# Rows ordered by expert, early lower gathers, and late tiles' results added onto base rows already stored in the output

## What is computed

```python
h = layernorm(x) * (1 + ca) + sa                      # sa .. gb: silu(c) @ wmod, six rows per batch
x = x + ga * rwkv_block(h)                            # time mix (K, V, R, O) and channel mix (key, silu, value)
h = layernorm(x) * (1 + cb) + sb
xt = h.reshape(2048, 512)
shared = sum_e gelu(xt @ Wsh_up[e]) @ Wsh_down[e]     # 2 shared experts, 512 -> 256 -> 512
probs = softmax(xt @ W_router)                        # 16 experts
top_v, top_i = top_k(probs, 2)
routed = sum_e gate[:, e] * (gelu(xt @ Wrt_up[e]) @ Wrt_down[e])
x = x + gb * (shared + routed)
```

## Time and profile before

| | us |
|---|---|
| median of 3 runs | 951.47 |
| the three runs | 957.27, 951.47, 950.63 |
| the profiled execution | 955.24 |
| its span, first to last instruction | 953.5 |
| granted TensorE clock, mean | 0.977 of 2.4 GHz |

### The profile page before, as it was taken

One profiled execution on the slowest core, in us unless ns is written; L12 is line 12 of the kernel. 1 busy time (PEld: TensorE's weight loads), 2 busy tenths in 40 slices (PEclk: granted clock), 3 DMA queues, 4 the chain that ended last, 5 costly groups with the idle time before them and its releaser, 6 DMA issues.

```text
span 953.5 us, 13516 instructions
## 1 busy us (share of the span) xinstructions
PE 894.7 (94%) x4264; PEld 720.3 (76%) x4265; DVE 531.9 (56%) x985; ACT 383.8 (40%) x632; POOL 382.5 (40%) x280
## 2 busy tenths in 40 slices
PE   7899779999998999998999999999999999999993
PEld 2457658788776888887888788878887888888772
DVE  5897897987657111356136513551684444444478
ACT  2566555573745542321222113225452333333441
POOL 2332200100022547227102610369527599897373
PEclk9899979999998999999999999999999999999997
DMA  9548578466056336153114411465435788776576
GB/s 357 188 132 263 193 221 262 156 202 195 1 189 213 109 109 205 40 166 131 55 34 152 135 67 34 162 229 177 161 126 180 249 262 271 237 275 235 163 256 203
DMA packets 105632, 166.69 MB, mean 175 GB/s; under 512 B 8152, under 2 KB 53208, under 8 KB 102512
## 3 DMA queue, kind: packets, MB, share of 16 engines
q1 hardware_dynamic: 59472, 112.59, 34.7%
q0 software_dynamic: 8960, 34.61, 11.4%
q10 hardware_dynamic: 37152, 18.88, 6.7%
HBM read 98.63 MB, written 67.42 MB: 174 GB/s over the span
## 4 chain that ended last, share of the span: by engine, by line
PE 70%; DVE 13%; DMA 6%; issue 4%; ACT 3%; POOL 2%; SPq 1%; another core or an unknown queue 1%; DVEq 0%; ACTq 0%
PE kk_ps L422 6%; PE kv_ps L422 6%; PE kk_ps L424 6%; PE kk_ps L423 6%; PE kv_ps L424 6%; PE kv_ps L423 6%; PE mm_ps L422 4%; PE mm_ps L423 4%; PE mm_ps L424 4%; PE up_ps L422 3%; DMA xsb<-xs_s 3%; PE dn_ps L422 2%; PE dn_ps L424 2%; PE dn_ps L423 2%; PE up_ps L423 2%
## 5 line engine op out<-in xcount | busy, mean ns | idle before, releaser
L1555 DVE TENSOR_TENSOR silu<-kk_ps,silu 128x512 fp32r<-128x512 f32 x64 | 44.2, 691 | 207.6 <-ACT silu L2162 193.2
L2158 ACT ACTIVATE kk_ps<-kk_ps 128x512 f32<-128x512 f32 x64 | 37.2, 582 | 214.9 <-PE kk_ps L424 199.9
L422 PE MATMUL kk_ps<-xk,cm_w 128*128 128x512 f32 x256 | 101.4, 396 | 0.0
L422 PE MATMUL kv_ps<-cm_w,silu 128*128 128x512 f32 x256 | 100.6, 393 | 0.0
L424 PE MATMUL kk_ps<-xk,cm_w 128*128 128x512 f32 x256 | 100.2, 391 | 0.0
L423 PE MATMUL kk_ps<-xk,cm_w 128*128 128x512 f32 x256 | 100.1, 391 | 0.0
L424 PE MATMUL kv_ps<-cm_w,silu 128*128 128x512 f32 x256 | 99.7, 390 | 0.0
L423 PE MATMUL kv_ps<-cm_w,silu 128*128 128x512 f32 x256 | 99.6, 389 | 0.0
L2325 POOL TENSOR_TENSOR cm_w<-stage,cm_w 128x1024 fp32r<-128x1024 f32 x16 | 38.7, 2424 | 90.4 <-ACT cm_w L1946 71.6
L2332 POOL TENSOR_TENSOR rs<-mv,neghalf 128x4 f32<-128x4 f32 (+2 forms) x13 | 13.5, 1038 | 145.3 <-DVE mv L1266 145.2
L2381 POOL TENSOR_TENSOR rs<-mv,neghalf 128x1 f32<-128x1 f32 x16 | 16.1, 1009 | 138.5 <-DVE mv L1580 138.5
(11 more groups left out here) (277 smaller groups left out, 2345.9 us busy)
## 6 DMA issues: line engine op xcount, KB each, us to landing
xs_s<-zero ACTq DMA_DIRECT2D x13, 1024.0 KB, 6.2
xsb<-xs_s SPq DMA_DIRECT2D x44, 256.0 KB, 4.0
ys_s<-ysb SPq DMA_DIRECT2D x41, 256.0 KB, 3.4
ex_raw<-in_wex POOLq DMA_DIRECT2D x9, 1024.0 KB
stage<-in_wcm SPq DMA_DIRECT2D x16, 512.0 KB, 3.9
wmod<-in_wmod SPq DMA_DIRECT2D x6, 1024.0 KB, 9.7
ex_raw<-in_wex SPq DMA_DIRECT2D x6, 1024.0 KB, 5.8
stage<-in_wtm SPq DMA_DIRECT2D x10, 512.0 KB, 6.3
```

The source lines that it names most:

```text
L422: pe.matmul(out, lhs[0], rhs[0], start=first, stop=False)
L1555: dve.tensor_tensor(silu[:, g % NSILU, 1, :], kk_ps[g % 2][:, :], silu[:, g % NSILU, 0, :].bitcast(F32), ALU.subtract).then_inc(s_silo, 1)
L2158: act.activation(kk_ps[g % 2][:, :], kk_ps[g % 2][:, :], ACT.Silu).then_inc(s_silu, 1)
```

## The change

1. The two rows of a token are ordered by expert instead of by rank: VectorE computes `spos` and reorders the gates (`by_expert`), from the kept first choices `top1`.
2. `last_tiles` writes how many increments the two store semaphores have when all tiles of experts 0 to 14 are stored. GpSimd waits for those and gathers the lower expert's rows of tiles 0 to 7 before `s_end`; after `s_end` the upper rows of tiles 0 to 7, then the lower rows of 8 to 15, then (after the first `up` block of batch 3) the upper rows of 8 to 15. ScalarE's `scaled` waits for a whole group of eight lower gathers (`gathered_lower`), VectorE for the tile's upper one.
3. `x4` of tiles 8 to 15 is stored in the output itself; the loads into `bsb` and VectorE's addition of it go, and each of these tiles leaves by an adding transfer from GpSimd. SyncE stores tiles 0 to 7 and at the end waits for those transfers.
4. All of `ys_s` is cleared: eight more clears of 1 MB, one in each of the steps g = 12 to 19 of the channel mix; the waits of SyncE and GpSimd on them count all 26.
5. The orders on ScalarE and VectorE in the tail are new.

The diff, without the buffers' declarations:

```diff
@@ -463,7 +460,10 @@
...
             before = 32 * NB if i < TT else 0 if i < TT + 2 else 16 * (NE - PRE) // 2
-            return before + 32 * (t // NG + 1)
+            return before + 16 * (t // NG + 1)
+
+        def gathered_lower(t):
+            return (s_base, 16 * (SB * TT + NG)) if t < NG else (s_bsl, 16 * (NB + NG))
...
@@ -728,7 +728,8 @@
...
                 sp.wait_ge(s_x4, t + 1)
-                sp.dma_start(x4_s[t], x4b[:, t % TT]).then_inc(s_x4st[t % TT], 16)
+                rows = x4_s[t] if t < SB * TT else out_d[t]
+                sp.dma_start(rows, x4b[:, t % TT]).then_inc(s_x4st[t % TT], 16)
...
@@ -802,7 +803,7 @@
...
             scatters_landed(NB - 1)
-            sp.wait_ge(s_zero, 16 * (2 * NSX - FULL) // 4)
+            sp.wait_ge(s_zero, 16 * 2 * NSX // 4)
             sp.wait_ge(s_tab, 1)
...
@@ -842,10 +843,11 @@
...
             sp.sem_inc(s_end, 1)
-            for t in range(NT):
+            for t in range(SB * TT):
                 sp.wait_ge(s_o4, t + 1)
                 sp.dma_start(out_d[t], g1b[:, t]).then_inc(s_out, 16)
-            sp.wait_ge(s_out, 16 * (NB + NT))
+            sp.wait_ge(s_out, 16 * (NB + SB * TT))
+            sp.wait_ge(s_bsl, 16 * (NB + NG + NT - SB * TT))
...
@@ -1618,8 +1620,9 @@
...
                 done(dve.tensor_tensor(lg[:, 1], lg[:, 1], per_expert(rev[:, :], TT), ALU.mult))
-                done(dve.tensor_reduce(top1[:, :], lg[:, 1], AX.X, ALU.max))
-                done(dve.tensor_tensor(oh[:, c], per_expert(rev[:, :], TT), per_token(top1[:, :], TT), ALU.is_equal))
+                first = top1[:, c, b * TT:(b + 1) * TT]
+                done(dve.tensor_reduce(first, lg[:, 1], AX.X, ALU.max))
+                done(dve.tensor_tensor(oh[:, c], per_expert(rev[:, :], TT), per_token(first, TT), ALU.is_equal))
...
@@ -1750,8 +1753,42 @@
...
                 done(dve.reciprocal(gates[:, 0], tops[:, :]))
-                dve.tensor_tensor(gates[:, 1].rearrange("p (t a) -> p t a", a=1), pr[:, :, NE:NE + 1],
-                                  gates[:, 0].rearrange("p (t a) -> p t a", a=1), ALU.mult).then_inc(s_gates, 1)
+                done(dve.tensor_tensor(gates[:, 1].rearrange("p (t a) -> p t a", a=1), pr[:, :, NE:NE + 1],
+                                       gates[:, 0].rearrange("p (t a) -> p t a", a=1), ALU.mult))
+
+            def by_expert():
+
+                w = pr[:, :, :].rearrange("p t e -> p (t e)")
+                lower, upper_ = w[:, 0:NT], w[:, NT:2 * NT]
+                at, p, q, o = (w[:, (2 + 2 * i) * NT:(4 + 2 * i) * NT].rearrange("p (c t) -> p c t", c=2)
+                               for i in range(4))
+
+                def both(v):
+                    return v.rearrange("p (a t) -> p a t", a=1).to_broadcast([P, 2, NT])
+
+                def ordered(v, out):
+                    own.up(dve.tensor_tensor(p, v, both(lower), ALU.mult))
+                    done(dve.tensor_tensor(q, v, both(upper_), ALU.mult))
+                    own.up(dve.tensor_tensor(out[:, 0], p[:, 0], q[:, 1], ALU.add))
+                    done(dve.tensor_tensor(out[:, 1], q[:, 0], p[:, 1], ALU.add))
+
+                dve.wait_ge(s_pos, NB)
+                own.up(dve.tensor_copy(at, pos[:, :, :]))
+                done(dve.tensor_tensor(lower, top1[:, 0], top1[:, 1], ALU.is_gt))
+                done(dve.tensor_scalar(upper_, lower, -1.0, 1.0, ALU.mult, ALU.add))
+                ordered(at, o)
+                own.up(dve.tensor_copy(spos[:, :, :], o))
+                ordered(gates[:, :, :], gates[:, :, :])
+
+            def last_tiles():
+
+                x = tends[0:1, NE - 2:NE - 1]
+                done(dve.tensor_scalar(total[:, :], x, 0.5, -0.25, ALU.mult, ALU.add))
+                done(dve.tensor_scalar(total[:, :], total[:, :], 8388608.0, None, ALU.add))
+                done(dve.tensor_scalar(total[:, :], total[:, :], -8388608.0, None, ALU.add))
+                done(dve.tensor_tensor(ecol[0:1, 0:1], x, total[:, :], ALU.subtract))
+                own.up(dve.tensor_scalar(tend[:, NE + 1:NE + 2], ecol[0:1, 0:1], 16.0, 16.0, ALU.mult, ALU.add))
+                dve.tensor_scalar(tend[:, NE + 2:NE + 3], total[:, :], 16.0, 16.0, ALU.mult, ALU.add)                    .then_inc(s_gates, 1)
...
@@ -1835,6 +1872,8 @@
...
             gates_b()
+            by_expert()
+            last_tiles()
             gb_shared(TT)
...
@@ -1882,6 +1921,7 @@
...
                 dve.wait_ge(s_o1, t + 1)
+                dve.wait_ge(s_gat[t % NG], gathered(t))
                 if t == 0:
...
@@ -1895,12 +1935,14 @@
...
                     dve.wait_ge(s_gsh, t + 1)
-                dve.wait_ge(s_bsl, 16 * (NT - SB * TT + NB))
+                dve.wait_ge(s_bsl, 16 * NB)
                 if t == 0:
                     dve.wait_ge(s_base, 16 * SB * TT)
-                base = base8[:, t] if t < SB * TT else bsb[:, t - SB * TT]
+                if t >= SB * TT:
+                    dve.tensor_tensor(g1b[:, t], g1b[:, t], gb2[:, b], ALU.mult).then_inc(s_o4, 1)
+                    return
                 done(dve.tensor_tensor(g1b[:, t], g1b[:, t], gb2[:, b], ALU.mult))
-                dve.tensor_tensor(g1b[:, t], g1b[:, t], base, ALU.add).then_inc(s_o4, 1)
+                dve.tensor_tensor(g1b[:, t], g1b[:, t], base8[:, t], ALU.add).then_inc(s_o4, 1)
...
@@ -1910,19 +1952,19 @@
...
             ht_lo(3, [0, 1])
+            combine([0])
             mid_lo(10)
             ht_lo(3, [2, 3])
-            combine([0])
+            combine([1])
             mid_lo(11)
-            combine([1, 2, 3, 4])
+            combine([2, 3, 4, 5, 6, 7])
             mid_lo(12)
-            combine([5])
             mid_lo(13)
-            combine([6])
+            combine([8])
             mid_lo(14)
-            combine([7])
+            combine([9])
             mid_lo(15)
-            combine(range(8, NT))
+            combine(range(10, NT))
...
@@ -2025,7 +2067,7 @@
...
-            groups = [(xs_s, q) for q in range(0, NSX, 4)] + [(ys_s, q) for q in range(FULL, NSX, 4)]
+            groups = [(xs_s, q) for q in range(0, NSX, 4)] + [(ys_s, q) for q in range(NSX - 4, -1, -4)]
...
@@ -2188,6 +2230,8 @@
...
                     weight_hi(14 + g)
+                elif 18 + g - 12 < len(groups):
+                    clear_slots(18 + g - 12)
                 if b and m in (4, 5):
...
@@ -2266,24 +2310,25 @@
...
                 for t in tiles:
-                    act.wait_ge(s_gat[t % NG], gathered(t))
+                    act.wait_ge(*gathered_lower(t))
                     act.activation(g1b[:, t], g1b[:, t], ACT.Copy, scale=gates[:, 0, t:t + 1]).then_inc(s_o1, 1)
-            gelu(2, [0, 1])
+            gelu(2, [0])
+            scaled([0, 1])
+            gelu(2, [1])
             ht_hi(3, [0, 1])
+            scaled([2])
             gelu(2, [2])
             ht_hi(3, [2, 3])
-            scaled([0])
+            scaled([3])
             gelu(2, [3])
-            scaled([1, 2, 3, 4])
+            scaled([4, 5, 6, 7, 8, 9, 10, 11])
             gelu(3, [0])
-            scaled([5])
+            scaled([12, 13])
             gelu(3, [1])
-            scaled([6])
+            scaled([14, 15])
             gelu(3, [2])
-            scaled([7])
             gelu(3, [3])
-            scaled(range(8, NT))
...
@@ -2368,7 +2413,7 @@
...
                 if b == 0:
-                    pool.wait_ge(s_zero, 16 * (2 * NSX - FULL) // 4)
+                    pool.wait_ge(s_zero, 16 * 2 * NSX // 4)
                 for t in range(b * TT, (b + 1) * TT):
...
@@ -2476,23 +2521,39 @@
...
-            expert_done(NE - ERING + 1)
-            pool.tensor_tensor(thr[:, 0:1], zero[:, 0:1], zero[:, 1:2], ALU.add)
+
+            def gather_lower(t):
+                pool.indirect_dma_start(g1b[:, t], None, ys_s,
+                                        bass.IndirectOffsetOnAxis(ap=spos[:, 0, t:t + 1], axis=0))\
+                    .then_inc(gathered_lower(t)[0], 16)
+
+            def gather_upper(t):
+                if t >= NG:
+                    pool.wait_ge(s_o4, t - NG + 1)
+                pool.indirect_dma_start(g2b[:, t], None, ys_s,
+                                        bass.IndirectOffsetOnAxis(ap=spos[:, 1, t:t + 1], axis=0))\
+                    .then_inc(s_gat[t % NG], 16)
+
+            pool.wait_ge(s_base, 16 * SB * TT)
+            for i in range(2):
+                stored = pool.value_load(tend[0:1, NE + 1 + i:NE + 2 + i], min_val=16, max_val=16 * NS + 16)
+                pool.wait_ge(s_yst[i], stored)
+                pool.tensor_tensor(thr[:, 1 + i:2 + i], zero[:, 0:1], zero[:, 1:2], ALU.add)
+            for t in range(NG):
+                gather_lower(t)
+            pool.wait_ge(s_end, 2)
+            pool.wait_ge(s_bsl, 16 * NB)
+            for t in range(NG):
+                gather_upper(t)
+            for t in range(NG, NT):
+                gather_lower(t)
+            pool.wait_ge(s_up, (NB - 1) * KT + 1)
+            for t in range(NG, NT):
```

(27 more changed lines are left out.)

## The result

| | before | after |
|---|---|---|
| median, us | 951.38 (7 runs) | 962.03 (7 runs) |
| lowest and highest | 949.78, 959.59 | 955.57, 967.04 |
| profiled execution | 955.24 | 962.9 |
| its span | 953.5 | 960.8 |

The ratio is 1.0097, 95% interval 1.0059 to 1.0135: slower by one per cent. The prediction was 948.7 us, range 944.0 to 955.5.

What follows compares the result with a forecast made beforehand. TensorE leads the chain at 70%, but VectorE sets the end. Profiled: 953.5 - 0.3 (bsb loads) - 5.3 (VectorE) + 2.8 (adding transfers) = 950.7, 2.8 less; from the median 951.47, 948.7 us, range 944.0 to 955.5.

Steps and rivals of the forecast that it cites:

- The tail behind VectorE: After VectorE's last operation: wake 0.3, adding transfer 4.5, closing 0.4; 5.2 us instead of 2.4, so +2.8.
- VectorE's sum: VectorE's tiles 8 to 15 take 2.11 us each instead of 2.85, ending at 945.8, 5.3 us before 951.06.
- rival E: Expert loop's end: early gathers delay the last stores, s_end 3 us later, knots move too; 951 to 952, chance 0.08.
- rival B: Tail: TensorE's 4 us stand costs its full clock, 1.7 us per stretch; 950.4 to 953, chance 0.14.
- The knots: Two places in the tail where ScalarE's scalings, ahead of gelus, wait for lower gathers; TensorE stalls 1.2 plus 1.0, then 4 us.
- First stall: scaled([0, 1]) ahead of gelu(2, [1]) on ScalarE: TensorE stalls 1.2 us, and mid_lo(11) costs another 1.0.
- Second: scaled(8..11) ahead of gelu(3, [0]) on ScalarE, lower gathers landing at 920.3: TensorE stands 4 us.
- The `bsb` loads: Eight loads beside the xsb load from 875.88 go: TensorE gains 0 to 0.5 us, taken as 0.3.
- Rival C: At the end adding transfers exceed 2.11 us each and queue up, costing 4.5 to 8 us; 953 to 957, chance 0.14.
- Price 0 for the clears and the small operations: Clears in the silu loop cost 0, at most 0.5 us; eighteen VectorE operations near 725 cost 0, at most 1.5.
- The early gathers: Eight lower gathers from 884.3 land by 897.5 beside the last two stores, putting upper gathers 0.7 us later, at 895.5.
- Chances: Whole kernel against a 9.5 us threshold: faster 0.07, slower 0.06 (above 961), the same 0.87.

Runs made afterwards that it cites:

- e1: Changed kernel with results of tiles 8 to 15 leaving by plain SyncE stores, their base rows left out: 957.03 us, ratio 1.0019.
- e2: Kernel before with one plain 2 KB GpSimd transfer issued after VectorE's last result: 960.73 us, ratio 1.0079.
- e0: Changed kernel again, with only a value-neutral mask of 127 on the word TensorE waits against in the expert loop: 965.64 us, ratio 1.0109.
- e11: Kernel before with the adding transfers for tiles 8 to 15 alone, gathers and orders as before: 959.51 us, ratio 1.0083.
- e7: Kernel before with only the eight more clears of ys_s: 954.58 us against 954.18, ratio 1.0006.
- e12: Kernel before with adding transfers for tiles 8 to 10 only, issued behind the last gather: 952.93 us, ratio 1.0023.
- e3: Changed kernel with gelu(3,[0]) ahead of scaled(8..11) on ScalarE: 962.72 us, ratio 1.0100.
- e8: Changed kernel with the eight early lower gathers behind the wait for all ys_s stores, ScalarE's order kept: 971.07 us, ratio 1.0178.
- e15: Kernel before with adding transfers for tiles 8 to 10, each issued behind the gathers of the tile four later: 949.44 us against 950.37, ratio 1.0003.
- e4: Changed kernel with all base rows added by VectorE from bsb as before, early gathers and orders as changed: 962.7 us, ratio 1.0107.

## Why the prediction was wrong, point by point

The prediction's sum on the profiled execution was -2.8 us; the two spans differ by +7.3. Of the 10.1 between them 4.3 lie behind VectorE's end, 5.5 at VectorE's end, and 0.3 are the gain for the `bsb` loads, which the sum had counted on top. Either of the first two alone would have left the time inside the range.

**The tail behind VectorE: the first step that failed.** "After VectorE's end come 5.2 us instead of 2.4", from 0.3 to wake, 4.5 to land and 0.4 of closing, took the landing for the last thing to end. The landing was not badly sized: 3.9 in the trace, 4.5 in the sum. What ended last was GpSimd's closing, 7.92 behind the last issue, 9.5 behind VectorE instead of my 5.2: +7.1 instead of +2.8. The row stands in the trace of before: I had read what follows VectorE's end, and not when each engine's queue closes. It was in no rival either. With e1 and e2 this is shown. By the Trainium skill, "DMA: Bandwidth & Descriptors", Anatomy of one DMA — SWDGE (gpsimd) path, the transfer would take 2.6 us, an estimate from that page's formula; the adding transfers of after took 3.9 in the median, so the trace does not agree, and it would not have changed the end.

**VectorE's sum: the second step.** The forecast was an end 5.3 us earlier than before; it came 0.2 later. Pitch 2.11 and the eight operations less were right. It ended at 951.24, not 945.8, for two reasons. `mid_lo(13)` ended at 930.8 instead of 927.3, since the upper gathers began at 898.96 instead of 895.5: 1.7 from the later loop (the half clock near 720, in no term of the sum), and 1.8 from the last store, which landed after 4.2 us beside the gathers instead of 2.06, rival E. And 2.1 us more it waited ahead of `mid_lo(14)`, behind half the clock, rival B, where the sum had 0.4 of waits. Both rivals had the mechanism and about the price (E 3 us, B 1.7); I had taken them as alternatives, and they came together.

**The knots.** First stall 0.98 and 0.88 instead of 1.2 and 1.0: right. Second 5.7 instead of 4, with the lower gathers landed at 924.2 instead of 920.3: right in kind in the profile of after, by its own chain. In e0, the same kernel, it is hidden by the stand at the loop's end.

**The `bsb` loads.** Forecast 0.3 gained; the loop was 0.5 us shorter from its first to its last copy, no more than it varies from profile to profile.

**Rival C** came nearest in size (953 to 957), at the wrong place. The adding transfers do not fall behind at 2.11 us: close together they land 1.3 us apart (e11). While they run the DMA engines are 0.92 busy, though, which I had put at a quarter.

**Price 0 for the clears and the small operations.** Not contradicted by the times (e7, whose interval reaches from -2.6 to +3.7 us); the clears cost a wait of 1.3 to 2.0 in the profile, over my 0.5.

**The early gathers.** Their benefit was priced and their cost was not, beyond the stores: a stand of TensorE in the expert loop, 3.6 to 5.4 us in seven of the eight profiles with all eight gathers early. It was absent from the first profile of after. From the parts, +7.1 for the closing, -1.2 to -1.5 at VectorE and +4.2 where the stand occurs make some 10, and the medians differ by 10.65. That the two agree is in part luck: what the executions without a profile held isn't recorded, and the profiled one of after, without the stand, was no faster than its median.

**Chances.** 0.06 for slower by over 1% was too small. Each step was bounded by rows of transfers, and none by what an engine does after its last instruction.

## What to carry to other kernels

Before a transfer is moved to an engine's queue near the end, read when that queue closes in the old trace: an issue there costs its closing too, here 7.9 us for a transfer of 256 KB and 8.0 for one of 2 KB. Work that has no one waiting for it (early gathers, clears) still has a price beside a loop in which TensorE never rests; look for it there before counting its benefit, and in more than one profile. Two rivals that hit the same buffer chain should be added before the range is drawn.

## What was not expected of the hardware

- GpSimd's queue closed 7.3 to 8.2 us after its last transfer was issued in fifteen of the seventeen profiles (a plain 2 KB transfer: 8.0). In e12 and e11, where the transfers landed late, it was 9.6 and 12.1. In seven profiles (e1, e3, e7, e8, e11, e12, e15) it closed 3.97 to 3.99 after the last GpSimd transfer of any kind had landed; in nine others 4.2 to 6.3 after, in e4 3.65, so the two figures together are no complete rule.
- Adding transfers of 256 KB into HBM at a pitch of 2.11: 3.9 us to land in after; 1.3 us apart in the row of eight of e11, issued close together.
- Beside indirect gathers the engines behind TensorE started late. In the expert loop ScalarE and VectorE began up to 7 us after the matmuls they waited for had ended by the record, most often some 3, and TensorE stood 3.6 to 5.4 us, in seven of eight profiles. With eight plain loads of the same size it did not (one profile). In the kernel before, one gelu beside the gathers began 2.2 us late. Why is not shown by any run here. Shorter stands of 1 to 2.9 us come in the later stretch of most kernels with the changed order of gathers, and are as open; the one of 2.7 us in e3 follows a gelu that began 4.7 us late.
